# Attention 2 of a four-layer stack: values with queries on the result's partitions, a column of ones as the softmax sum, one projection per batch

## What is computed

```
# 16 heads of 8 features, E = 128; x: (4, 512, 128), ctx: (4, 154, 128)
n = layernorm(x)
q = n   split in heads @ Wq.T       # Wq, Wk, Wv: 8 x 8, the same for all heads
k = ctx split in heads @ Wk.T
v = ctx split in heads @ Wv.T
p = softmax(q k.T * 128**-0.5 + mask)     # per head, 512 x 154
x = x + concat(p v) @ Wo.T + bo
```

## Time and profile before

| | |
|---|---|
| median of 3 runs | 1284.26 us (1276.24 to 1287.08) |
| span of the profiled execution | 1241.1 us, 43.2 us under the median |
| TensorE busy, weight loads busy | 1028.2 us (83%), 793.3 us (64%) |
| VectorE, ScalarE, GpSimd busy | 756.0 us (61%), 658.9 us (53%), 670.2 us (54%) |
| mean granted clock of TensorE | 0.892 of 2.4 GHz |
| attention 2, its loop of 16 stages | about 281 to 446 us |

### The profile page before, as it was taken

How to read it: one execution, slowest core, us unless ns; L and a number is a source line. 1 busy time by engine, 2 the same in 40 slices (tenths; PEclk the granted TensorE clock), 3 DMA queues, 4 the chain that set the end, 5 groups by cost and what they waited for, 6 DMA issues and landing times.

```text
span 1241.1 us, 22522 instructions
## 1 busy us (share of the span) xinstructions
PE 1028.2 (83%) x6547; PEld 793.3 (64%) x6547; DVE 756.0 (61%) x2570; ACT 658.9 (53%) x2366; POOL 670.2 (54%) x1163
## 2 busy tenths in 40 slices
PE   3984999847899977986999998397699999966993
PEld 3874788734555547774677765386467776645993
DVE  4367254587878776247676687532776676754443
ACT  2225233337888952446887875243387888831321
POOL 5122456546666745257655565647475555655452
PEclk9775899977999995998999999599789999975998
DMA  3422446684920021420000000166300000014566
GB/s 60 4 27 89 131 155 208 202 145 164 389 84 2 2 69 35 136 78 1 19 1 18 18 2 18 41 178 186 96 18 2 1 1 2 2 35 124 172 203 196
DMA packets 132377, 102.82 MB, mean 83 GB/s; under 512 B 34651, under 2 KB 113939, under 8 KB 132256
## 3 DMA queue, kind: packets, MB, share of 16 engines
q1 hardware_dynamic: 121360, 82.38, 24.1%
q0 software_dynamic: 8448, 17.20, 4.2%
q10 hardware_dynamic: 2448, 1.80, 0.6%
HBM read 64.98 MB, written 36.36 MB: 82 GB/s over the span
## 4 chain that ended last, share of the span: by engine, by line
PE 53%; DVE 18%; issue 8%; POOL 8%; ACT 7%; DMA 5%; SPq 1%; DVEq 0%; ACTq 0%; POOLq 0%
PE ps L2645 5%; PE ps L2826 4%; PE ps L2647 4%; PE ps L2646 4%; PE ps L2840 4%; PE ps L2705 3%; ACT ex L1377 3%; DMA xr<-xr_d,src_i 2%; PE ps L2720 2%; POOL yq_d L884 2%; PE ps L2854 2%; POOL pp L1050 2%; PE ps L3318 2%; PE ps L3137 2%; ACT ex L1263 2%
## 5 line engine op out<-in xcount | busy, mean ns | idle before, releaser
L1050 POOL TENSOR_TENSOR pp<-ex,rc 128x256 f32<-128x256 f32 x384 | 236.1, 615 | 202.9 <-DVE rc L2178 144.9
L1263 ACT ACTIVATE ex<-ps,nmx 128x154 f32<-128x154 f32 x512 | 193.9, 391 | 70.5 <-DVE nmx L2173 69.2
L2173 DVE TENSOR_REDUCE nmx<-ps 128x2 f32<-128x308 f32 x256 | 119.4, 469 | 62.3 <-PE ps L2647 61.9
L884 POOL DMA_INDIRECT yq_d<-yq,ids_q x78 | 74.7, 957 | 75.4 <-DVE yq L1908 56.4
L2826 PEld LDWEIGHTS ps<-ident,pp 128*128 128x128 f32 x640 | 74.0, 142 | 57.5 <-POOL pp L1051 49.9
L1377 ACT ACTIVATE ex<-ps,nmx 128x154 f32<-128x154 f32 x256 | 97.4, 393 | 22.9 <-DVE nmx L2038 22.5
L2645 PE MATMUL ps<-kp,q_s 128*128 128x308 f32 x256 | 96.5, 377 | 15.1 <-ACT ex L1263 8.1
L1051 POOL TENSOR_TENSOR pp<-ex,rc 128x52 f32<-128x52 f32 x384 | 105.9, 276 | 0.0
L1263 ACT ACTIVATION_READ_ACCUMULATOR ex<-ps,nmx 128x1 f32 x512 | 105.0, 205 | 0.0
L2826 PE MATMUL ps<-ident,pp 128*128 128x128 f32 x640 | 100.5, 281 | 4.7 <-POOL pp L1051 4.7
L854 POOL TENSOR_TENSOR ln_r<-ln_v,mhalf 128x4 f32<-128x4 f32 x32 | 34.5, 1079 | 88.3 <-DVE ln_v L1659 76.8
(11 more groups left out here) (441 smaller groups left out, 2806.4 us busy)
## 6 DMA issues: line engine op xcount, KB each, us to landing
w_r<-in_L_ffn_W SPq DMA_DIRECT2D x69, 256.0 KB, 3.5
xq_d<-blankq SPq DMA_DIRECT2D x4, 4160.0 KB, 24.5
w_q<-in_L_ffn_W SPq DMA_DIRECT2D x46, 256.0 KB, 3.4
w_q<-in_L_ffn_w SPq DMA_DIRECT2D x46, 128.0 KB, 2.7
xq<-xq_d SPq DMA_DIRECT2D x22, 130.0 KB, 2.2
w_s<-in_L_ffn_W SPq DMA_DIRECT2D x8, 256.0 KB, 7.0
w_e<-in_L_ffn_W SPq DMA_DIRECT2D x8, 256.0 KB, 4.9
acc<-yq_d SPq DMA_DIRECT2D x8, 256.0 KB, 4.5
```

The source lines that it names most:

```text
L884: pool.indirect_dma_start(yq_d[:, :], bass.IndirectOffsetOnAxis(ap=ids_q[:, c:c + 1], axis=0), yq[k % NY][:, h, :], None).then_inc(q_out[k ...
L1050: pool.tensor_tensor(pp[st % 2][:, m % 4, 2 * j:2 * j + 2, :], w[:, :, 0:P], r.broadcast_to([P, 2, P]), ALU.mult)
L1263: ins = act.activation(ex[:, tt % NEX, j, :], ps[:, tt % 3, j * SK:(j + 1) * SK], ACT.Exp, bias=nmx8[:, tt % 8, j:j + 1], accum_out=sm8[:, ...
L2173: dve.tensor_reduce(nmx8[:, tt % 8, :], ps[:, tt % 3, 0:2 * SK].rearrange("p (h s) -> p h s", h=2), AX.X, ALU.max, negate=True).then_inc(n ...
```

## The change

- The exponentials go unnormalised into `pe1`, a tile per stage parity, without the accumulator. The reciprocals and GpSimd's products are gone. GpSimd copies the last 26 keys of all heads together (`pr1`); transposes 0 to 3 read `pe1` and wait for ScalarE, transpose 4 waits for GpSimd's copy.
- The values get a ninth column of ones per head (`vv1`, `vr1`, the latter zero outside its own head by the block matrix `blk`). The turned probabilities become the stationary operand: 16 products of 128x128 by 9 columns, and 4 of 128x128 by 36 for the rest. The result has the queries on partitions, and column 9 of each head is the softmax sum.
- VectorE takes 16 reciprocals in one instruction, multiplies, and writes the group's part of `acc`, now rows (`normalise`). Nothing is projected until all four groups of a batch are there.
- Then per batch: four transposes (`turned_out`), one ScalarE copy, four FP32 products with the turned Wo (`project`), which give rows, and the addition to the residual. Batches 0 and 1 fall into stages 14 and 15, 2 and 3 behind the loop.
- bo is loaded to all partitions and added to the residual by GpSimd before. Wo is loaded by one transfer and turned by TensorE (`("w", 0)`, `wo1`).
- Later attentions keep their own arithmetic; only the offsets of their semaphore counts change. The mask's staging tiles move to another place.

```diff
+    BEHIND1 = {(14, "C"): [("o", 0)], (15, "A"): [("f", 0)], (15, "C"): [("o", 1)]}
+    TAIL = [("pt", NST - 1, 1), ("f", 1), ("pt", NST - 1, 3), ("pt", NST - 1, 2), ("o", 2), ("pt", NST - 1, 4), ("t", 0), ("f", 2), ("t", 1), ("o", 3), ("f", 3), ("t", 2), ("t", 3)]
...
+            names += [("pt", st - 1, 1)] * late + [("prep", st // B + 1, st % B)] * (B <= st < NST - B) + BEHIND1.get((st, "A"), [])
+            names += [("pt", st - 1, 2), ("pt", st - 1, 3)] * late + BEHIND1.get((st, "C"), [])
...
+        vv1 = [over(f"vv1{u}", [P, B, 4, 9], F32, vv_at[u])[0] for u in range(2)]
+        vr1 = [over(f"vr1{u}", [P, B, 4, 9], F32, vr_at[u])[0] for u in range(2)]
+        oT1 = [over(f"oT1{u}", [P, S], F32, pt_at + 2048 * (4 + u))[0] for u in range(2)]
+        pe1 = [at(f"pe1{u}", [P, TB, 4, SK], F32, (56832, 74240)[u]) for u in range(2)]
+        pr1 = [at(f"pr1{u}", [P, TB, 4, 32], F32, (44544, 67072)[u]) for u in range(2)]
+        wo1 = at("wo1", [P, P], F32, 49664)
...
+            sp.dma_start(bo1[:, :], t["L1_xattn_bo"].rearrange("(a d) -> a d", a=1).broadcast_to([P, D])).then_inc(in_vec, 16)
...
-            for j in range(4):
-                for g in range(4):
-                    h = 4 * g + j
-                    sp.dma_start(woP[rows * j:rows * j + dh, g, :],
-                                 t["L1_xattn_Wo"][:, dh * h:dh * h + dh].rearrange("e d -> d e"), allow_slow_non_contiguous=True).then_inc(in_l1, 16)
+            sp.dma_start(woP[:, 0, :], t["L1_xattn_Wo"]).then_inc(in_l1, 16)
...
+                        pool.memset(pr1[u][:, :, :, SK - P:], 0.0)
+                        pool.memset(vv1[u][:, :, :, 8:9], 1.0)
+                        ins = pool.tensor_copy(vr1[u][:, :, :, 8:9], blk[:, :].rearrange("p (a h c) -> p a h c", a=1, c=1).broadcast_to([P, B, 4, 1]))
...
-                    normalise(0, 0)
-                    normalise(0, 1)
-                    normalise(0, 2)
-                    normalise(0, 3)
                     rstd(2, 3)
-                    normalise(0, 4)
-                    normalise(0, 5)
-                    normalise(0, 6)
-                    normalise(0, 7)
+                    for b in range(B):
+                        pool.wait_ge(ln_ok, B * 2 + b + 1)
+                        pool.tensor_tensor(x_tok[:, tiles(b), :], x_tok[:, tiles(b), :], bo1[:, :].rearrange("p (a d) -> p a d", a=1).broadcast_to([P, TB, D]), ALU.add).then_inc(p_add, 1)
                     pool.memset(blankq[:, :, 0:D + 1], 0.0)
                     pool.memset(blankq[:, :, D + 1:D + 2], float(2 * (SPARE + NRUN * RUN))).then_inc(q_blank, 1)
-                if l > 1:
-                    rstd(2 * l, 0)
-                    rstd(2 * l, 1)
-                    low_x(0)
-                    rstd(2 * l, 2)
-                for st in range(1 if l == 1 else 0, NST):
+                    for st in range(NST):
+                        if st >= 2:
+                            pool.wait_ge(*full(l, ("pt", st - 2, 4)))
+                        pool.wait_ge(n_e, 8 * st + 8)
+                        pool.tensor_copy(pr1[st % 2][:, :, :, 0:SK - P], pe1[st % 2][:, :, :, P:SK]).then_inc(n_pr, 1)
+                    return
...
+                        if m == 0 and st >= 2:
+                            act.wait_ge(*full(l, ("pt", st - 2, 4)))
                         act.wait_ge(n_m, tt + 1)
-                        wait(act, n_z, tt - NEX + 1)
                         for j in range(2):
-                            ins = act.activation(ex[:, tt % NEX, j, :], ps[:, tt % 3, j * SK:(j + 1) * SK], ACT.Exp,
-                                                 bias=nmx8[:, tt % 8, j:j + 1], accum_out=sm8[:, tt % 8, j:j + 1])
+                            ins = act.activation(pe1[st % 2][:, m % 4, m // 4 * 2 + j, 0:SK], ps[:, tt % 3, j * SK:(j + 1) * SK], ACT.Exp, bias=nmx8[:, tt % 8, j:j + 1])
...
-                def high_out(st):
-
-                    if 0 <= st < NST:
-                        act.wait_ge(n_pv, st + 1)
-                        if st:
-                            act.wait_ge(*full(l, ("y", st - 1)))
-                        act.activation(oT1[0][:, :], ps[:, 5 + st % 2, :], ACT.Identity).then_inc(n_oh, 1)
+                def turned_out(b):
+
+                    act.wait_ge(*full(l, ("o", b)))
+                    if b >= 2:
+                        act.wait_ge(*full(l, ("f", b - 2)))
+                    act.activation(oT1[b % 2][:, :], ps[:, bank_of(l, ("o", b)), :], ACT.Identity).then_inc(n_fa, 1)
...
+                            ins = dve.tensor_tensor(vr1[u][:, :, :, 0:8], rows, blk[:, :].rearrange("p (a h c) -> p a h c", a=1, c=1).broadcast_to([P, B, 4, 8]), ALU.mult)
...
-                    if 0 < tt <= 8 * NST:
-                        dve.wait_ge(n_e, tt)
-                        wait(dve, n_z, tt - 8)
-                        dve.reciprocal(rc8[:, (tt - 1) % 8, :], sm8[:, (tt - 1) % 8, :]).then_inc(n_r, 1)
...
-                def low_out(st):
+                def normalise(st):
                     if 0 <= st < NST:
-                        dve.wait_ge(n_oh, st + 1)
-                        dve.tensor_tensor(oT1[1][:, :], ps[:, 5 + st % 2, :], oT1[0][:, :].bitcast(F32), ALU.subtract).then_inc(n_ol, 1)
-
-                def add_up(st):
-
-                    if 0 <= st < NST:
-                        cols = bsl(st % B)
-                        dve.wait_ge(*full(l, ("y", st)))
-                        if st >= B:
-                            dve.wait_ge(*drained(l, RING[l][0]["y", st - B]))
-                        y = ps[:, bank_of(l, ("y", st)), :]
-                        if st < B:
-                            ins = dve.tensor_scalar(acc[:, cols], y, bo1[:, 0:1], None, ALU.add)
-                        else:
-                            ins = dve.tensor_tensor(acc[:, cols], acc[:, cols], y, ALU.add)
-                        ins.then_inc(n_fd, 1)
+                        g, b = st // B, st % B
+                        dve.wait_ge(n_pv, st + 1)
+                        rows = ps[:, 5 + st % 2, 0:TB * 36].rearrange("p (k h c) -> p k h c", k=TB, h=4)
+                        link(dve.reciprocal(rc1[:, :, :].rearrange("p k (h c) -> p k h c", c=1), rows[:, :, :, 8:9]))
+                        dve.tensor_tensor(acc[:, bsl(b)].rearrange("p (k g h c) -> p k g h c", k=TB, g=4, h=4)[:, :, g, :, :], rows[:, :, :, 0:8],
+                                          rc1[:, :, :].rearrange("p k (h c) -> p k h c", c=1).broadcast_to([P, TB, 4, 8]), ALU.mult).then_inc(n_on, 1)
...
-                    elif i == 2:
+                    else:
+                        w = wP[2][:, gs].rearrange("p (h c) -> p h c", h=4)[:, :, 0:8]
                         for b in range(B):
-                            last = mm(ps[:, bank, b * P:(b + 1) * P], ctxT[:, b * SK:b * SK + P], wP[2][:, gs], start=True, stop=True)
-                    else:
-                        for h in range(4):
-                            for b in range(B):
-                                last = mm(ps[32 * h:32 * h + 32, bank, b * 32:(b + 1) * 32], ctxT[:, b * SK + P:b * SK + P + 32],
-                                          wP[2][:, g * P + 32 * h:g * P + 32 * h + 32], start=True, stop=True)
+                            if i == 2:
+                                last = mm(ps[:, bank, b * 32:(b + 1) * 32].rearrange("p (h c) -> p h c", h=4), ctxT[:, b * SK:b * SK + P], w, start=True, stop=True)
+                            else:
+                                for h in range(4):
+                                    last = mm(ps[32 * h:32 * h + 32, bank, b * 32:(b + 1) * 32].rearrange("p (h c) -> p h c", h=4), ctxT[:, b * SK + P:b * SK + P + 32], w, start=True, stop=True)
...
-                    pe.wait_ge(n_z, 8 * st + (4 if c < 2 else 8))
+                    if c < 4:
+                        pe.wait_ge(n_e, 8 * st + (4 if c < 2 else 8))
+                    else:
+                        pe.wait_ge(n_pr, st + 1)
                     bank = slot(("pt", st, c))
                     for k in range(TB):
-                        last = pe.transpose(ps[:, bank, k * P:(k + 1) * P], pp[st % 2][:, k, c, :], ident[:, :])
+                        keys = pe1[st % 2][:, k, c, 0:P] if c < 4 else pr1[st % 2][:, k, :, :].rearrange("p h c -> p (h c)")
+                        last = pe.transpose(ps[:, bank, k * P:(k + 1) * P], keys, ident[:, :])
...
-                    wait(pe, n_ol, st - 1)
+                    wait(pe, n_on, st - 1)
                     if st == 0:
                         pe.wait_ge(xT_ok, B * s + B)
                     for h in range(4):
-                        last = mm(ps[32 * h:32 * h + 32, 5 + st % 2, :], vv1[g % 2][:, b, 32 * h:32 * h + 32], pt_s[h][:, :], start=True, stop=False)
+                        for k in range(TB):
+                            at_ = 36 * k + 9 * h
+                            last = mm(ps[:, 5 + st % 2, at_:at_ + 9], pt_s[h][:, k * P:(k + 1) * P], vv1[g % 2][:, b, h, :], start=(h == 0 and k == 0), stop=False)
```

(67 more changed lines are left out.)

134 lines of the change are left out of this document (66 added, 68 removed).

## The result

The changed kernel takes 1327.3 us (1325.0 to 1327.5); the kernel before, run beside it, 1280.8 (1276.2 to 1287.1). The ratio is 1.035, with a 95% interval of 1.031 to 1.040: slower by 46 us. I had forecast +97. The direction and the bound (TensorE's loads, made dearer by a lower clock) were right, the size was twice too large.

What follows compares the result with a forecast made beforehand. No engine was full; a ring of waits bound attention 2, TensorE idling 1.4 us a stage for GpSimd. Afterwards TensorE's loads bind: loop +86, preparation +8, head -1, tail +4 make +97, about 1380 us, range 1325 to 1430.

Steps and rivals of the forecast that it cites:

- The price of a pass: Values block of attention 2: one small pass takes 0.11 us at 2.4 GHz, 0.22 at 1.2 GHz.
- TensorE as the bound: Attention 2's loop: TensorE busy without a gap, ScalarE and VectorE half busy, GpSimd nearly empty.
- The stage at 2.4 GHz: One stage of attention 2's loop takes 10.0 us if the clock doesn't fall.
- What brings the clock down: Values block, 3.6 us of nine-column products a stage: such thin passes lower the clock even without idle gaps.
- The tail: Attention 2's last addition to the residual: old steps go, values and projections come, +4 us (-3 to +9).
- Head and loads: Before the loop: smaller VectorE copies of values, -1 us; one Wo load for 16 issues, 0.
- The step that failed: Attention 2's loop: clock falls in most stages, returning at the earliest after the last scores with the query product.
- 16.0 as the mean: Mean stage of attention 2's loop in us, ends 12.5 and 20.5; fifteen values blocks give +86 us.
- my middle case: Stage of attention 2 where the clock comes back just for the values block: 17 us.
- it falls only now and then: Rival, chance 0.10: clock falls where the values block lies badly; stages 11 to 12 us, total 1300 to 1320.
- The preparation's +8: Preparing groups' keys and values in the loop no longer hides behind other work: +8 us (0 to +12).
- The base: Profiled span 1241.1 us plus 43.2 us around it taken as the kernel before's median, 1284.26 us.

Runs made afterwards that it cites:

- earlier trace: Profile of the kernel before that the prediction read, no edit; span 1241.1 us, listed runs' median 1284.26 us.
- second pair of traces: The kernel before and the changed kernel, both unedited, profiled again on the experiments' chips: 1245.0 and 1296.7 us.
- split block: Changed kernel with the 32 passes of values cut by head into four pieces between scores and transposes; 1252.4 us, ratio 1.005 to the kernel before.
- second trace: Changed kernel, unedited, profiled again on the experiments' chips; 1296.7 us, ratio 1.039 to the kernel before.
- first trace: First profile of the changed kernel, unedited, from the result's measurement: 1327.3 us, ratio 1.035 to the kernel before.
- earlier preparation: Changed kernel with the next keys prepared one step earlier on TensorE, ScalarE and VectorE, values block whole; 1300.5 us, ratio 1.041 to the kernel before.
- filled blocks: Changed kernel with 16 wide bf16 products added between each stage's 16 products of values; 1291.8 us, ratio 1.033 to the kernel before.
- half the passes: Changed kernel with probabilities and values of the large products in fp32r, 16 passes a stage for 32; 1248.9 us, ratio 1.003 to the kernel before.

## Why the prediction was right and wrong

**What held.** The price of a pass: 0.11 and 0.21 to 0.22 from the earlier trace rows, 0.109 and 0.213 measured, and 0.11 in fp32r at 2.4 GHz. TensorE as the bound: 94% busy in the loop, the others half empty. The stage at 2.4 GHz: 10.0 in the sum, 10.2 to 10.3 in the undisturbed stages, 9.8 with the block cut. What brings the clock down, told from the earlier trace rows: 307.6 to 310.9 repeats what 61.4 had shown. The tail: +4, measured +4.4 and +4.6. Head and loads, -1 and 0: in the second pair of traces the first query products stand at 273.2 and 273.1, so nearly nothing.

The Trainium skill (TensorE: Matmul & The Clock Gate, section Why this matters for your kernels) has the clock drop after gaps and stay for back-to-back matmuls. The stretch from 413.4 lost it behind a gap too, but one of 1.84 us, shorter than the gaps that the section warns of; the one from 307.6, 3.30 of 3.30 us busy, speaks against the rule. The split block has the same products, no less back to back, and the clock at 1.00 from 292.8 to 443.6, so what differed is how many thin products stand in one piece.

**The step that failed** is how long the clock stays down: "I expect the clock to fall in most stages inside or just behind this block, and to come back at the earliest after the densest piece", and from it "16.0 as the mean". The first half held: of the thirteen stages from 306.20 to 475.84 it fell in eight (about 311, 332, 345, 362, 393, 407, 417 and 448 us), all but two times inside or just behind a block. The second half did not: it was back after 3.0 to 10.5 us, and low for about 57 of these 170 us, where my middle case has it low for 13 to 14 of every 17. Six of the stages kept it or nearly, at 10.6 on average; the seven others took 15.1, and not 17. Most blocks ran at 2.4 in full, as that of 377.82 did. The mean is 13.0, and the loop costs +43.6 to +48.2, not +86. In the second trace the falls are fewer and longer, up to some 20 us, and the share is much the same. The pieces around a block are dense, as the earlier trace rows had shown, and that may be why the clock comes back so soon; no run here shows it. I gave this only the chance of a rival. That rival, "it falls only now and then" (11 to 12 us a stage), came nearer than my forecast, and the truth lies between the two.

Two smaller terms. The preparation's +8 is in the loop's figure and can't be told from it; with the clock held (the split block) the whole loop is only 2.3 us longer, so at 2.4 GHz it is nearly nothing: its longer stages take 10.4 to 10.8 us, those of the kernel before 11.2 to 11.3. And the hole of 1.8 us that VectorE's keys make is a second way for the clock to fall that I saw in the kernel before but did not carry over: in the first trace the three blocks that ran at 1.2 GHz throughout stand behind it. The earlier preparation showed that it adds nothing that shows as long as the block is whole; the filled blocks showed that it matters once they are cured.

**The base**: 43 us around the span was no such thing, but, as it seems, an execution quicker than the listed runs. It cancels in the difference; it would not have if I had scaled by it.

What stays open: which stages keep the clock, and for how long it is down. Two traces of the changed kernel lose it in different stages, and no run here says what decides it for one block.

## What to carry to other kernels

Turning a product so that its large operand becomes stationary costs one 128x128 load a pass, 0.10 to 0.12 us at 2.4 GHz for all moving widths from 8 to 36 columns here: 32 loads (3.5 us) for 4 wide products (1.0 us). Count the loads before the flops. If the thin products must be, put them in small pieces between wide ones: the same instructions cut in four took about 43 us less. Before summing against a span, see that its run is one of those that the median speaks of.

## What the runs showed of the hardware

- A wide bf16 product between thin ones is nearly free: 16 of 308 columns lengthened a quiet stage by 0.6 us, 0.04 each, though the same form takes 0.14 among the scores (305.90 to 306.04 in the first trace). In the block, a thin product of two passes with its wide neighbour takes 0.27 us (438.19 to 438.46), without it 0.22.
- A thin fp32r product of ten columns takes the time of one of two fp32 passes, about 0.11 us; it halves the block (quiet stages go from 10.3 to 8.4 us).
- The clock falls in two ways, each seen without the other: behind nine-column products without a gap (311.0 in the first trace, 427.4 with the keys prepared earlier), and behind a wait of 1.84 us (all four in the filled blocks; with half the passes two of three, the wait of 1.83 us that ends at 366.4 didn't do it). Eight such passes in a piece (the split block, from 292.8 to 443.6) or sixteen of fp32r (half the passes, from 336 to 379) did not bring it down.
- The kernel before took 1281 us in the runs beside the result and 1245 to 1248 in those of the experiments, with attention 2's loop at 164.6 us in both traces. Between the two traces of the changed kernel the loop accounts for none of the 31 us between their spans (208.2 and 212.8 us); 12.4 us of them stand before the loop and some 18 in the experts from 882.5.
